# Attention: the second head's weights of each pair of heads are turned by VectorE and DRAM instead of TensorE, and summed one pair later

## The reference, cut to what matters

```python
q = xn @ Wq                       # 8 batches x 256 tokens, 16 heads x 64
k, v = split(xn @ Wkv)            # one key and value head for all 16
k, v = [null_k, k], [null_v, v]   # one more key in front
s = -(q @ k.T) * scale + bias[h] + mask + causal
p = softmax(s, axis=-1)
out = (p @ v).reshape(tokens, 16 * 64) @ Wo
```

## Time and profile before

| | |
|---|---|
| time, median of 3 runs | 850.19 us (842.87 to 850.97) |
| span of the profiled execution | 793.7 us, 16690 instructions |
| own time of the profiled execution | not given apart from the three runs; the span and about 56.5 us around it make the median |
| busy in the span | PE 94%, PEld 75%, DVE 57%, ACT 48%, POOL 53% |
| stage c, first to last weighted sum | 347.8 to 654.8 us |
| mean clock granted to TensorE | 0.972 of full speed |

### The profile page before, as it was taken

How to read it: one execution, slowest core, us unless ns; L and a number is a source line. 1 busy time by engine, 2 the same in 40 slices (tenths; PEclk the granted TensorE clock), 3 DMA queues, 4 the chain that set the end, 5 groups by cost and what they waited for, 6 DMA issues and landing times. The chain is left out here.

```text
span 793.7 us, 16690 instructions
## 1 busy us (share of the span) xinstructions
PE 748.7 (94%) x4993; PEld 595.9 (75%) x4994; DVE 453.7 (57%) x1647; ACT 381.9 (48%) x1094; POOL 422.4 (53%) x506
## 2 busy tenths in 40 slices
PE   8889999769999999989999999999999988899998
PEld 4479966549999999867777777777777754699965
DVE  0824475672232323356666787778878787256557
ACT  3556612242222222166666565656666651777611
POOL 1077327525554852274656668686868356056640
PEclk9999999759999999999999999999999999999999
DMA  9636635429897773395000000000000001356547
GB/s 323 279 108 191 137 118 160 126 81 342 309 329 273 223 231 121 107 401 174 28 1 28 2 28 29 28 29 28 29 1 29 1 29 63 102 160 177 153 149 236
DMA packets 57022, 106.36 MB, mean 134 GB/s; under 512 B 8816, under 2 KB 42864, under 8 KB 55792
## 3 DMA queue, kind: packets, MB, share of 16 engines
q1 hardware_dynamic: 40368, 55.96, 20.9%
q0 software_dynamic: 10944, 30.03, 12.5%
q10 hardware_dynamic: 5632, 19.41, 7.2%
HBM read 78.31 MB, written 27.07 MB: 133 GB/s over the span
## 5 line engine op out<-in xcount | busy, mean ns | idle before, releaser
L2135 POOL TENSOR_TENSOR work<-work,region_ac 128x386 f32<-128x386 f32 x128 | 120.3, 945 | 67.2 <-DVE work L1797 32.7
L1683 ACT ACTIVATE work<-work 128x129 f32<-128x129 f32 (+1 forms) x256 | 114.0, 449 | 5.8 <-DVE work L1797 5.8
L1797 DVE CUSTOM_DVE_ANT_0 work<-psH,work 128x129 f32<-128x129 f32 (+1 forms) x256 | 78.8, 345 | 2.6 <-PE psH L1482 2.6
L1690 ACT COPY work<-psHT 128x384 f32<-128x384 f32 x64 | 30.6, 479 | 86.4 <-PE psHT L1492 86.4
L1355 POOL DMA_INDIRECT d_pairs<-work,home x47 | 46.1, 981 | 42.8 <-DVE home_f L1107 27.4
L1463 PE MATMUL psY<-work,region_ac 128*128 128x256 f32 x256 | 66.9, 384 | 0.5 <-ACT work L1677 0.5
L1516 PE MATMUL psM<-region_ac,work 128*128 128x256 f32 x256 | 66.0, 380 | 0.0
L1025 ACT ACTIVATE work<-work 128x512 f32<-128x512 f32 x39 | 24.6, 630 | 86.0 <-DVE work L1044 86.0
L1344 POOL DMA_INDIRECT b_pairs<-work,home x39 | 38.0, 975 | 49.8 <-DVE work L1051 46.8
L1336 POOL DMA_INDIRECT work<-in_x,inv x39 | 37.0, 949 | 47.0 <-DVE inv L1264 35.5
L848 PE MATMUL psH<-work,region_bd 128*128 128x128 f32 x472 | 59.2, 280 | 2.0 <-ACT region_bd L747 1.1
(11 more groups left out here) (368 smaller groups left out, 1694.6 us busy)
## 6 DMA issues: line engine op xcount, KB each, us to landing
region_bd<-in_b_w ACTq DMA_DIRECT2D x37, 512.0 KB, 5.4
work<-d_rows SPq DMA_DIRECT2D x47, 132.0 KB, 2.2
a_slots<-work SPq DMA_DIRECT2D x19, 256.0 KB, 2.9
region_bd<-in_b_w SPq DMA_DIRECT2D x1, 4096.0 KB, 15.3
work<-b_pairs SPq DMA_DIRECT2D x16, 256.0 KB, 3.1
region_bd<-in_d_w SPq DMA_DIRECT2D x1, 4096.0 KB, 13.2
work<-d_pairs SPq DMA_DIRECT2D x16, 256.0 KB, 4.3
d_rows<-region_bd SPq DMA_DIRECT2D x1, 2112.0 KB, 28.5
```

What stands on the lines that cost most here:

```text
L1683: nc.scalar.activation(c_p[:, o, a:z], c_sc[:, o, a:z], ACT.Exp, scale=-1.0, bias=c_min[:, o, i:i + 1], accum_out=c_sum[:, j % 2, o, i:i + ...
L1797: last = nc.vector.tensor_tensor_reduce(c_sc[:, o, a:z], psH[:, o, a:z], c_bm[:, 2 * (j % 2) + o, a:z], 1.0, -LOWEST, ALU.add, ALU.min, c_ ...
L2135: pool.tensor_tensor(c_bm[:, 2 * (j % 2) + o, :], c_mp, c_bias[:, 2 * j + o, :], ALU.subtract).then_inc(C.bm_ready, 1)
```

## The change

The weights of head 0 are turned by PE as before, those of head 1 no longer. DVE transposes the 128x384 weights of head 1 in squares of 32x32 (`dve_blocks`), which leaves each square turned in its own quadrant of 32 partitions. SP then stores the tile to DRAM and loads it back with the squares' places exchanged, in four loads of 32 partitions each (`sp_blocks`). Since that takes time, the weighted sums and the output product of a pair come one pair later (LAG = 2), with doubled buffers for the spread reciprocals, the turned weights and the values. Head 1 is now taken before head 0 everywhere (ORDER). The null key of the second half of the queries moves to the end, so that three whole squares lie together. The expert weights of stage d are loaded in 36 pieces, one after each pair's loads; their second bias, whose place the new buffers take, is loaded when the last product is done. Some work of DVE and POOL on the last batch's results comes one iteration later.

```diff
+BLOCK = QT * P + P
+ORDER = (1, 0)
+LAG = 2
...
         def pe_turn(pe, p):
-            for o in range(2):
-                pe.wait_ge(C.p_ready, 4 * p + 2 * o + 2)
-                wait(pe, C.pT_ready[o], p)
-                for n, at in enumerate((1, KEYS0 + 1, KEYS0 + 1 + P)):
-                    last = pe.transpose(psHT[:, o, n * P:(n + 1) * P], c_p[:, o, at:at + P], ident[:, :])
-                last.then_inc(C.p_turned, 1)
+            pe.wait_ge(C.p_ready, 4 * p + 4)
+            wait(pe, C.pT_ready, p - 1)
+            for n in range(QT + 1):
+                last = pe.transpose(psHT[:, p % 2, n * P:(n + 1) * P], c_p[:, 0, 1 + n * P:1 + (n + 1) * P], ident[:, :])
+            last.then_inc(C.p_turned, 1)
         def pe_sum(pe, p, j, b):
-            for s in C.pT_ready:
-                pe.wait_ge(s, p + 1)
+            pe.wait_ge(C.pT_ready, p + 1)
+            wait_dma(pe, C.blocks_loaded, 0, p)
...
...
             for j in range(NPAIR):
                 p = 8 * b + j
                 more = not (last and j == NPAIR - 1)
-                act_pT(act, p)
                 if more:
-                    act_exp(act, p + 1, j + 1, 0)
+                    act_exp(act, p + 1, j + 1, ORDER[0])
+                act_pT(act, p)
                 act_queries(act, p + 2, j, not (last and j + 2 >= NPAIR))
                 if more:
-                    act_exp(act, p + 1, j + 1, 1)
+                    act_exp(act, p + 1, j + 1, ORDER[1])
...
-        def dve_pT(dve, p):
-            dve.wait_ge(C.p_turned, 2 * p + 2)
-            wait(dve, C.pv_mm, p)
-            nc.vector.tensor_copy(c_pT[:, 1, :], psHT[:, 1, 0:3 * P]).then_inc(C.pT_ready[1], 1)
+        def dve_blocks(dve, p):
+            dve.wait_ge(C.p_ready, 4 * p + 2)
+            if p >= 2:
+                wait_dma(dve, C.blocks_stored, 0, p - 2)
+            nc.vector.transpose(out=c_x1[:, p % 2, :, :, :].rearrange("p b i q -> p i b q"),
+                                in_=c_p[:, 1, 1:1 + BLOCK].rearrange("p (i b q) -> p i b q", b=4, q=32)).then_inc(C.blocks_turned, 1)
...
+        def sp_load_d(sp, p):
+            if p < 16:
+                sp.dma_start(d_w13[:, p, :, :], io["d_w13"][:, p, :, :]).then_inc(D.weights_loaded, 16)
+            elif p < 32:
+                sp.dma_start(d_w2[:, p - 16, :], io["d_w2"][:, p - 16, :]).then_inc(D.weights_loaded, 16)
...
+        def sp_blocks(sp, p):
+            r = p % 2
+            sp.wait_ge(C.blocks_turned, p + 1)
+            if p >= 2:
+                wait_dma(sp, C.blocks_loaded, 0, p - 2)
+            sp.dma_start(blocks_dram[r], c_x1[:, r, :, :, :].rearrange("p b i q -> p (b i q)")).then_inc(C.blocks_stored.sems[r], 16)
+            wait_dma(sp, C.blocks_stored, 0, p)
+            wait(sp, C.pv_mm, p - 1)
+            stored = blocks_dram[r].rearrange("(a k) (b m) -> b k a m", a=4, b=4)
+            for b in range(4):
+                sp.dma_start(c_x2[32 * b:32 * b + 32, r, :, :, :].rearrange("p a i q -> p a (i q)"), stored[b]
+                             ).then_inc(C.blocks_loaded.sems[r], 16)
...
+            for p in range(NPAIR * BATCH):
+                b, j = divmod(p, NPAIR)
+                sp_blocks(sp, p)
+                sp_load_d(sp, p)
+                if j == 4 and b + 2 < BATCH:
+                    sp_pairs(sp, b + 2)
+            sp.wait_ge(C.o_ready, NPAIR * BATCH)
+            load_broadcast(sp, d_b2, "d_b2", D.weights_loaded)
```

More of the change, by code:

```diff
@@ L1481, in pe_scores @@
                     half = slice(DH * o, DH * o + DH)
[L1482 removed]
+                    last = pe.matmul(psH[:, o, a:z], c_qr[half, j % 2, i * P:(i + 1) * P], c_kT[half, i:i + z - a],
                                      start=True, stop=True)
@@ L1501, in pe_sum @@
             wait(pe, C.o_ready, p)
-            for n, keys, queries in ((0, 0, slice(0, SEQ)), (1, 1, slice(P, SEQ))):
-                at = slice(n * SEQ, n * SEQ + queries.stop - queries.start)
+            weights = (c_pT[:, p % 2, :].rearrange("p (i a q) -> p i a q", a=4, q=32), c_x2[:, p % 2, :, :, :].rearrange("p a i q -> p i a q"))
+            for n, queries, blocks in ((0, slice(0, SEQ), slice(0, QT)), (1, slice(P, SEQ), slice(QT, QT + 1))):
                 for o in range(2):
-                    last = pe.matmul(psL[DH * o:DH * o + DH, queries], c_v[:, keys, :], c_pT[:, o, at],
-                                     start=(n == 0), stop=(n == 1))
+                    last = pe.matmul(psL[DH * o:DH * o + DH, queries].rearrange("p (i a q) -> p i a q", a=4, q=32),
+                                     c_v[:, b % 2, n, :], weights[o][:, blocks, :, :], start=(n == 0), stop=(n == 1))
             last.then_inc(C.pv_mm, 1)
@@ L1611, in pe_batch @@
                 p = 8 * b + j
-                before = not (first and j == 0)
-                if before:
-                    pe_sum(pe, p - 1, (j - 1) % NPAIR, b - (j == 0))
+                s = p - LAG
+                if s >= 0:
+                    pe_sum(pe, s, s % NPAIR, s // NPAIR)
                 if not (last and j == NPAIR - 1):
@@ L1687, in act_pT @@
         def act_pT(act, p):
-            act.wait_ge(C.p_turned, 2 * p + 1)
-            wait(act, C.pv_mm, p)
-            nc.scalar.copy(c_pT[:, 0, :], psHT[:, 0, 0:3 * P]).then_inc(C.pT_ready[0], 1)
+            act.wait_ge(C.p_turned, p + 1)
+            wait(act, C.pv_mm, p - 1)
+            nc.scalar.copy(c_pT[:, p % 2, :], psHT[:, p % 2, 0:BLOCK]).then_inc(C.pT_ready, 1)
         def act_zT(act, b):
@@ L1781, in dve_v @@
             dve.wait_ge(C.kv_mm, b + 1)
-            wait(dve, C.pv_mm, 8 * b)
-            nc.vector.scalar_tensor_tensor(out=c_v, in0=values_x[:, :, 0:DH], scalar=-float(DH) ** 0.5,
+            wait(dve, C.pv_mm, 8 * (b - 1))
+            nc.vector.scalar_tensor_tensor(out=c_v[:, b % 2, :, :], in0=values_x[:, :, 0:DH], scalar=-float(DH) ** 0.5,
                                            in1=nvb[:, :].unsqueeze(1).to_broadcast([P, QT, DH]), op0=ALU.mult, op1=ALU.add
@@ L2036, in dve_batch @@
                 p = 8 * b + j
+                s = p - LAG
                 more = not (last and j == NPAIR - 1)
-                if not (first and j == 0):
-                    dve_o(dve, p - 1, j + 1)
+                dve_blocks(dve, p)
+                dve_sums(dve, p, j)
+                dve_over(dve, p)
                 dve_dispatch_start(dve, b, j, last)
+                if s >= 0:
+                    dve_o(dve, s, s % NPAIR)
                 if j == 0 and not first:
@@ L2098, in dve_attention @@
             dve_scores_wait(dve, 0)
-            for o in range(2):
+            for o in ORDER:
                 dve_scores(dve, 0, 0, o)
             batches(dve, dve_batch)
+            dve_o(dve, NPAIR * BATCH - 2, NPAIR - 2)
             dve_o(dve, NPAIR * BATCH - 1, NPAIR - 1)
@@ L2205, in pool_batch @@
                 over = (j + 2) // NPAIR
-                for o in range(2):
-                    h = 2 * j + o
+                for n, o in enumerate(ORDER):
+                    h = 2 * j + n
                     if h <= 2 * QT and not last:
                         pool_pairs_wait(pool, b + 1, h)
-                    if j == 4 and o == 0:
+                    if j == 4 and n == 0:
                         pool.wait_ge(C.xn_ready, 2 * b + 2)
-                    if j == 6 and o == 1 and not first:
+                    if j == 6 and n == 1 and not first:
                         pool.wait_ge(C.z_step, 2 * b)
@@ L2346, in _ @@
             sp.wait_ge(fB.turned, 4 * RING)
-            sp.dma_start(c_bias[:, :, KEYS0 + 1:KEYS], bias[1]).then_inc(C.loaded, 16)
+            sp.dma_start(c_bias[:, :, KEYS0:KEYS - 1], bias[1]).then_inc(C.loaded, 16)
             sp_attention(sp)
@@ L2492, in _ @@
             dve_attention(dve)
+            dve.wait_ge(D.weights_loaded, D.loads + 16)
             dve_ffn_pairs(dve, fD)
```

162 lines of the change are left out of this document (86 added, 76 removed).

## The result

The changed kernel takes **874.49 us** (median of 4 runs, 869.82 to 882.66), the kernel before 847.49 (4 runs, 842.87 to 850.97): ratio **1.0351, 95% interval 1.0264 to 1.0437** (the two medians alone give 1.0319), slower. The forecast was 846 us, 831 to 872. The rival "SP becomes the bound" had 873 us and a chance of 0.15.

A forecast was written before the change was run, and what follows sets the result against it. PE was taken to bound the kernel at 4.41 us per light pair, with a DVE and ACT loop of 4.33 us taking over. Attention stage -7 and last trip +3 gave -4 from 850.2: 846 us, range 831 to 872.

The forecast's parts named there:

- SP becomes the bound: Rival: SP's wait for the store's landing sets the attention stage's pace, rounds 5.4 and 4.9 us; 873 us, chance 0.15.
- part 5: Trip through DRAM on SP's queue: 5.6 us under 8.2 us, SP's round 4.5 us; free except +3 us at the end.
- the new average of 4.76: Forecast mean period per pair in us, heavy pairs included, that SP's round of 4.5 us was held against.
- Part 1: Three turns fewer on PE per pair: 0.30 us off, light period 4.41 to 4.11 us, worth 19.2 us if PE binds.
- Part 2: New order makes a loop through DVE and ACT of 4.33 us, longer than PE's 4.11, 0.08 under today's 4.41.
- Part 3: Pairs with extra work add 4.3 us to eight loops, 38.9 us a batch; 300 us for 63 periods against 307.
- The -7: Forecast change of the attention stage's 63 periods in us: 300 against 307, before the cost of the last trip.
- the rival of POOL: DVE's spread waits more often for POOL, loop 0.18 us longer, 11 us over 63 periods: 857 us, chance 0.15.
- The +3 for the last trip: End of the attention stage: last sum waits about 5.6 us where before 2.6, costing 3 us, 2 to 5.
- Part 4: DVE's transpose of head 1's weights: 0.50 us, hidden in six pairs of eight, ends -4 and +6 us.
- The estimate of 0.93: Alternative time in us for DVE's transpose, three squares at 311 ns each; it would raise the sum some 6 us.

The follow-up runs named there:

- wact_key_order: Changed kernel with weight pieces issued from ACT's queue, router's key first on DVE, next scores ahead of spread and product: ratio 1.000 to the kernel before, 63 periods 301.4 us.
- no_trip: Changed kernel without the store to DRAM and four loads, PE reading DVE's squares directly: ratio 1.013 to the kernel before, 63 periods 312.9 us.

## Why the prediction was wrong

**The step that failed is in part 5: "SP's own round is 2.0 + 5 x 0.48 + 0.1 = 4.5 us, under the new average of 4.76, in 36 pairs ... It costs nothing as long as those hold."** Two things were wrong in it. The landing of 2.0 is that of a store with nothing ahead of it in its queue, and here a store stands behind a weight piece: 3.16 us behind 256 KB, 2.32 behind 128 KB, 1.92 behind none. So the round was 5.6 us in the first 16 pairs. The issues were right: 1.74 for four loads, 0.43 for a piece. And the comparison with the average was wrong: the buffers hold two pairs, so a round has to fit the light pairs (4.3 to 4.5 in the loop), not a mean that the heavy ones lift; the round of 4.7 with small pieces still bound. Price of both, from one edit: 21.9 us. The second alone shows with the pieces of 128 KB: there the round is 4.7 at the median, under the 4.76, and the 63 periods are still 14.3 us longer than with the pieces in ACT's queue (321.0 for 306.7). The rival named the right place (a round of 5.4, +20) and the point from which it decides, a landing of 2.3, but I set aside as measured "beside heavy traffic", when the change itself puts such traffic, a 256 KB piece, ahead of each store. That its 873 us lies so near the measured 874.49 is in part luck: it had rounds of 5.4 in 36 pairs and 4.9 in the others, where the medians are 5.6 in pairs 1 to 15 and 4.9 in the 16 behind them, and it had neither the key nor the later start.

**Part 1 held.** PE's shortest usual period is 4.09, forecast 4.11.

**Part 2 held in kind.** PE lost its place as the bound to the loop of DVE and ACT. In the kernel with the pieces in ACT's queue the round without anything extra on DVE (iteration 1) is 4.32, forecast 4.33; iterations 6 and 7 are 4.47 and 4.51.

**Part 3 was sized too small.** Forecast 38.9 a batch, measured 39.7 (6.39 and 5.83 in iterations 3 and 4), and 306.7 us for 63 periods where I had 300. The -7 became 0: three turns less on PE bought nothing in this order; with the scores moved up as well (wact_key_order) they bought 5.1 to 6.6 us of the stage. Part of it is the spread on the path, the rival of POOL; its instruction in the changed kernel (busy, mean ns) was

```profile
L1828 DVE COPY region_bd<-work 128x256 f32<-128x256 f32 x64 | 33.7, 527 | 2.2
```

527 ns for 457 in the earlier trace rows. In the kernel of the 306.7 us it is 500, so 63 x 0.04 = some 2.7 us of the 7 that are missing, by my estimate; that rival had priced it at 11. The Trainium skill ("SBUF — State Buffer", who interferes with whom) says that such a copy and a POOL instruction exclude each other for a whole instruction; the 1.26 us above agrees. The rest of the 7 lies in the heavy iterations, 39.7 a batch for 38.9.

**What I did not see.** The router's key had moved behind the transpose, the reciprocal and the spread; the diff shows it, and no term of the sum was made for it: 2.9 us in the changed kernel, 5.8 where SP didn't hide it. And sums one pair later cost 3.5 to 5.5 us at the stage's start (9.1 to 11.1 from the first scores to the first sum for 5.6), since no sum can begin until a pair more has been prepared.

**The +3 for the last trip was near in size, and mostly not the trip's.** The wait lies ahead of the last sum, so it is part of the 63 periods. In the profile after:

```profile
708.56 0.31 PEld L1505 LDWEIGHTS psHT<-ident,work 128*128 128x128 f32 x3 [1.40 <-ACT work L1700]
...
714.81 0.13 PEld L1518 LDWEIGHTS psL<-work,region_bd 128*64 128x64 f32 x1 [1.66 <-issue]
```

From the last turns to the last sum 6.2 us pass, on the page of before 2.3 (651.97 to 654.29), 3.9 more. But PE stands only 1.66 us before that sum, where 0.33 is usual, so about 1.3 us are the trip's. The rest is the later place of the sums: without any trip, in no_trip, the same way takes 5.1 (687.48 to 692.54).

**Part 4 held, its estimate from a page didn't.** The transpose in the profile after:

```profile
L1837 DVE STREAM_TRANSPOSE region_bd<-work 128x384 f32<-128x384 f32 x64 | 36.6, 572 | 5.7 <-ACT work L1700 4.5 <-DMA c_blocks<-region_bd 0.9 <-issue 0.2
```

0.57 us, forecast 0.50. The estimate of 0.93 from the Trainium skill ("VectorE: DVE Perf Modes", the three transpose paths) was too long by more than half: the page has 311 ns for one bf16 square of 128x128, and here three such squares of float32 in one instruction take 190 ns each.

**The sum, put right**: 21.9 for the pieces, 2.9 for the key, 0 for loop and turns, 5.1 at the start, 0.8 behind the last sum: 31. The profiled executions give 331.5 - 308.0 + 10.7 - 5.6 + 157.5 - 156.7 = 29.4; the 1.3 between the two are the loop and turns, 306.7 for 308.0. The medians give 27.0 (874.49 less 847.49) and, in the second group, 28.0 (873.88 less 845.89). The 0.8 has no cause here: that stretch alone varies by more.

**Open.** Why two executions of the kernel before differ by 46.6 us outside the stage. The lower granted clock goes with it, but no run shows how much of it that explains. How the 21.9 us divide between the landing and the piece's issue. What in the heavy iterations makes up the rest of the 7 us.

## What to carry to other kernels

When a DMA has to land before the next step, count what its own queue was given just before it as part of its landing, and move bulk loads to another queue. Compare a server's round with the shortest interval that the buffers let it see, not with an average. An engine that catches up shows its own pace, not the bound's: read the period on the loop that waits for itself.

## What the runs showed of the hardware

A store of 192 KB to DRAM let its reader go 1.92, 2.32, 3.16 and 18.35 us after its issue, with nothing, 128 KB, 256 KB, and 6.8 MB of weights with 2.1 MB of rows ahead of it in its queue; with 256 KB pieces in another queue it was 2.6 at the median. A copy of 128x256 float32 values on DVE, 0.29 us at the median of the kernel before, took 1.26 where POOL had an instruction of 1.01 us in the same time. A DMA issue on ACT (0.33 us) ran beside ACT's own instruction. A transpose in squares of 32 of 128x384 float32 values took 0.57 us on DVE. After a stretch of 6.3 us in which PE was busy for 3.73, and stood for at least the 1.6 us up to 611.4, its clock was granted at half from 611.6 to 618.2.
